# Issuing the broadcast of the layer-0 MLP gate ahead of the last two groups' query and value transfers

## The reference

```
tp = silu(cond) @ Wt + bt                     # 128 sequences x 6*128
shift_msa, scale_msa, gate_msa, shift_mlp, scale_mlp, gate_mlp = split(tp)
h = layernorm(x) * (1 + scale_msa) + shift_msa
x = x + gate_msa * attention(h)               # 16 heads of 8, 32 tokens each
h = layernorm(x) * (1 + scale_mlp) + shift_mlp
x = x + gate_mlp * (gelu(h @ W1 + b1) @ W2 + b2)
```

## Time and profile before

| | |
|---|---|
| runs | 303.29, 306.14, 344.91 us |
| span of the profiled execution | 302.6 us |
| that execution's own device time | not recorded apart; the lowest of the runs is 0.7 us above its span |
| TensorE busy | 260.4 us, 86% |
| VectorE, ScalarE, GpSimd busy | 201.6, 175.8, 185.6 us |
| DMA queue q1 | 51600 packets, 15.80 MB |
| MLP gate broadcast | four DMAs of 512 KB, 12.5 us median from issue to landing |
| V store, V read | 288 KB in 2.4 us, 72 KB in 2.6 us, medians |

### The profile page before, as it was taken

How to read it: one execution, slowest core, us unless ns; L and a number is a source line. 1 busy time by engine, 2 the same in 40 slices (tenths; PEclk the granted TensorE clock), 3 DMA queues, 4 the chain that set the end, 5 groups by cost and what they waited for, 6 DMA issues and landing times.

```text
span 302.6 us, 7656 instructions
## 1 busy us (share of the span) xinstructions
PE 260.4 (86%) x2524; PEld 201.1 (66%) x2524; DVE 201.6 (67%) x620; ACT 175.8 (58%) x366; POOL 185.6 (61%) x195
## 2 busy tenths in 40 slices
PE   0768629689999979858999999979999889999996
PEld 0556519487777766538777777858767557777776
DVE  5998964938999999816454555698999855453002
ACT  2266735646987975680555555487766696555330
POOL 5744274735687677619778788887777544445410
PEclk9999986959999999995999999999999999999999
DMA  7952766424245245670000000000000001111112
GB/s 229 320 171 33 144 107 148 90 52 85 62 66 102 61 69 98 123 140 2 1 0 0 0 0 0 2 0 2 1 0 0 1 1 37 35 35 35 35 37 69
DMA packets 52200, 18.09 MB, mean 60 GB/s; under 512 B 32464, under 2 KB 51152, under 8 KB 52048
## 3 DMA queue, kind: packets, MB, share of 16 engines
q1 hardware_dynamic: 51600, 15.80, 24.4%
q10 hardware_dynamic: 576, 1.98, 2.0%
HBM read 11.35 MB, written 4.59 MB: 53 GB/s over the span
## 4 chain that ended last, share of the span: by engine, by line
PE 50%; DMA 15%; DVE 13%; issue 7%; ACT 7%; SPq 4%; POOL 1%; DVEq 1%; ACTq 0%; POOLq 0%
PE bank L1069 20%; PE bank L931 14%; DMA values_scratch<-Vs 7%; PE bank L961 5%; DMA gate<-gates_scratch 4%; PE bank L906 3%; DMA Vx<-values_scratch 3%; ACT Kx L752 3%; DVE stats L444 2%; SPq L238 2%; SPq L253 2%; DVE hA L473 2%; PE bank L974 2%; DMA X<-x 2%; ACT xhat L737 1%
## 5 line engine op out<-in xcount | busy, mean ns | idle before, releaser
L737 ACT ACTIVATE xhat<-X,shift,rstd 128x128 f32 (+1 forms) x96 | 39.4, 483 | 56.7 <-POOL shift L294 56.6
L1069 PE MATMUL bank<-W,Qx 128*128 128x128 f32 x512 | 62.0, 282 | 0.0
L1069 PEld LDWEIGHTS bank<-W,Qx 128*128 128x128 f32 x512 | 61.0, 199 | 1.0 <-issue 1.0
L931 PE MATMUL bank<-h,W 128*128 128x512 f32 x128 | 58.5, 595 | 0.5 <-ACT Qx L787 0.5
L305 POOL TENSOR_TENSOR h<-hA,B 128x512 f32<-128x512 f32 x32 | 33.5, 1047 | 26.4 <-DVE hA L473 26.1
L473 DVE TENSOR_TENSOR hA<-bank,A 128x512 f32<-128x512 f32 x32 | 22.0, 688 | 39.5 <-PE bank L906 16.2
L787 ACT ACTIVATE Qx<-bank,col 128x512 f32<-128x512 f32 x64 | 39.3, 678 | 8.8 <-PE bank L931 8.8
L292 POOL TENSOR_TENSOR rstd<-v_sb,minus_half 128x4 f32<-128x4 f32 x32 | 32.6, 1018 | 17.8 <-DVE v_sb L464 13.2
L961 PE MATMUL bank<-Kx,Qx 128*128 128x128 f32 x256 | 37.3, 292 | 4.7 <-DVE Qx L607 1.3
L931 PEld LDWEIGHTS bank<-h,W 128*128 128x128 f32 x128 | 22.8, 191 | 22.0 <-issue 20.3
L961 PEld LDWEIGHTS bank<-Kx,Qx 128*128 128x128 f32 x256 | 32.8, 201 | 6.5 <-DMA Qx<-Qs 1.7
(11 more groups left out here) (124 smaller groups left out, 445.5 us busy)
## 6 DMA issues: line engine op xcount, KB each, us to landing
values_scratch<-Vs SPq DMA_DIRECT2D x8, 288.0 KB, 2.4
Vx<-values_scratch SPq DMA_DIRECT2D x32, 72.0 KB, 2.6
gate<-gates_scratch SPq DMA_DIRECT2D x8, 256.0 KB, 6.6
gate<-gates_scratch SPq DMA_DIRECT2D x4, 512.0 KB, 12.5
Qx<-Qs SPq DMA_DIRECT2D x28, 64.0 KB
out<-X SPq DMA_DIRECT2D x7, 256.0 KB, 2.3
W<-weights ACTq DMA_DIRECT2D x1, 1152.0 KB, 6.2
X<-x SPq DMA_DIRECT2D x4, 256.0 KB, 7.2
```

The source lines that it names most:

```text
L737: last = act.activation(xhat[:, p, P * t:P * (t + 1)], X[:, x_tile(gg, t), :], ACT.Identity, bias=shift[:, p, t:t + 1], scale=rstd[:, p, t ...
L931: last = pe.matmul(bank[2 + n][:, :], w(f"W1_{phase // 2}", n), h[:, p, :], start=True, stop=True)
L1069: last = pe.matmul(y[t // 2][:, P * t:P * (t + 1)], gT[:, p, n, P * t:P * (t + 1)], w(f"W2_{phase // 2}", n), start=(n == 0), stop=(n == N ...
```

## The change

The call that issues the MLP gate's four DMAs moves from behind the V round trip of group 7 to right behind the loop, ahead of the V round trip of group 6, the query copy of group 7 and the V round trip of group 7. Nothing else is altered: the same DMAs, waits and semaphores, and the waits for `gates_in[2]` on VectorE and GpSimd stay where they are.

```
                 spread_q(i * 2 + 4, 0)
+            spread_gates(2, 1, slice(0, NT))
             spread_v(6, 0, 3)
             spread_q(7, 1)
             spread_v(7, 1, 3)
-            spread_gates(2, 1, slice(0, NT))
```

## The result

The changed kernel takes 312.75 us (median of 4 runs, 311.0 to 313.73) against 305.3 us before (median of 4). The ratio is 1.030, 95% interval 1.025 to 1.036: slower by some 9 us. The ratio leaves out disturbed runs such as the one of 344.91 us before, and so it is not the quotient of the two medians. The forecast was 312.5 us, in a range of 305.5 to 317, slower with 0.80.

A forecast was written before the change was run, and what follows sets the result against it. V round trips were taken to bound phase 0, the MLP gate the seam, then TensorE: 14.2 us late less 6.0 regained is +8.2, span 302.6 to 310.8, with 0.7 around it 311.5; forecast 312.5 us, range 305.5 to 317.

The forecast's parts named there:

- Group 6's values come later: Late phase 0: group 6's V store waits for the gate data, landing at 117.2 instead of 104.35, 12.85 us late.
- The clock at that gap: TensorE behind the wait for group 6's values: half clock costs 2.0 us, 1.4 net of an absorbed 0.70 us wait.
- The query copy and the store of group 7 hide: End of phase 0: group 7's query copy lands by 125.5, its scores come at 127.3, so no cost.
- The seam gives back 6.0 us: Start of phase 1: the gate in time saves 3.2 us of wait and 2.8 us of slow clock.
- The sum: Whole kernel: 14.2 us late at weighting 7, less 6.0 us regained at the seam, gives 8.2 us slower.
- B: Group 6's store: only SP's 10.12 us of issue delays it, 7.1 us; kernel 2.5 us slower; chance 0.07.
- C: Group 6's store: issues take about 2.2 us, data leave it room, nothing late; kernel 6.0 us faster; chance 0.07.
- D: Seam to phase 1: something else holds its start, nothing is regained; kernel 14.2 us slower; chance 0.08.

The follow-up runs named there:

- split_late: Kernel before, with the MLP gate still behind group 7's V round trip but in two calls with a semaphore each: 297.34 us against 304.49, ratio 0.980.
- half_early: Kernel before, with half of the MLP gate issued right behind the loop, the other half behind group 7's V round trip: 304.51 us against 304.49.
- sp_held: Kernel before, with SP waiting, queue empty, ahead of group 6's V round trip until about 107.5; run again: 310.34 us against 304.01, ratio 1.024.
- act_queue: Kernel before, with the MLP gate's four DMAs on ScalarE's queue, two ahead of its group 5, two ahead of group 6: 315.45 us against 304.49.

## Why the prediction was right

It was right in its size and by its own steps, with one wrong idea of what makes the store wait.

**Group 6's values come later.** Forecast 12.85 us, measured 123.00 - 108.80 = 14.2. The term was 1.35 too small, mostly because the gate's data took 19.7 us and not 18.6 (the fourth DMA, issued at 102.35, landed 15.3 us later), while the store's lag behind them was 0.7 us as against 0.6. SP's hold was forecast at 10.12 us and was 9.83.

**The clock at that gap.** Weighting 6 to weighting 7 took 12.29 us against 11.28, so 1.0 net of the absorbed wait; forecast 1.4. The first 5.19 us (to the next group's scores) compare with 3.62, so 1.6 and not 2.0. A gap of 15.5 us cost no more clock than one of 6, as I had assumed.

**The query copy and the store of group 7 hide.** They did: the scores that need the copy did not wait, and the wait for group 7's values was 0.25 us.

**The seam gives back 6.0 us.** Measured 5.9: from weighting 7 to `hA` 13.01 us against 16.11, from `hA` to `up` 5.04 (153.34 in the chain of waits) against 7.80. It was also shown alone (split_late). What I split into 3.2 of wait and 2.8 of clock is not two separate sums: with the wait kept, the clock was worth 1.7.

**The sum.** 14.2 + 1.0 - 5.9 = 9.3 us, the difference of the spans; forecast 8.2. That 312.5 us came within 0.3 us of the median is luck, of errors that cancel. The sum was 1.1 us too small for the profiled execution, and the time around the span, 1.8 us in each of the four runs, was taken as 0.7. Against these 2.2 us stand 1.0 that I had put on top of the sum toward the high median, and 1.0 by which the profiled execution lies above the median of the four. With the 1.8 us the sum on my own terms would have been 312.6.

**The rivals.** B (only SP is held) falls by half_early, where SP is free in 2 us and the store still takes 7.8, and by sp_held, where the hold alone accounts for 6 of 14 us. C needed SP free and the data out of the store's way, and neither was so. D falls by the rows of the seam.

**What was wrong.** I wrote that a store waits for the gate data "queued before it", and thought of SP's one queue. Half of the gate on ScalarE's queue held group 6's store for as long as the same half on SP's (7.9 and 7.8 us). The figure was not touched by this, since the rows behind it held either way, but the remedy that the idea suggests cost 11 us when it was tried (act_queue).

## What to carry to other kernels

A large transfer issued early is free only if no transfer on the chain is issued while it is under way, on whatever queue; look up what the next small transfer behind it has for slack, and what the same pattern did to its neighbours elsewhere in the trace. Where a bulk transfer is waited for as a whole and only its first part is needed, split it in two with a semaphore each and leave it where it is: that took the same wait away here for nothing. What must go in between is best cut into pieces as long as the gaps. Lay out what one broadcast moves with its rows close together, in the scratch and in SBUF.

## What the runs showed of the hardware

- Two megabytes of broadcast took 19.7 us in runs of 512 B and about 13 us in runs of 16 KB with the rows closer together; for the attention gate the closer rows alone took the median from 6.6 to 5.0 us, and the longer runs from there to 4.9.
- The Trainium skill, DMA: Bandwidth & Descriptors, "Anatomy of one DMA", has 2.0 us plus bytes over 436 GB/s, an estimated 6.8 us for the 2.1 MB; neither 19.7 nor 13 comes near. The page gives that fit for DMAs that GpSimd issues, and these came from SP, so it was a weak rule to hold against the rows, in the prediction too.
- A transfer on SP's queue was held by DMAs issued on ScalarE's: a query copy's four issues took 7.00 instead of 2.6 us, a store 7.9 us to land instead of 2.4 to 3.3. The same page, "Issuing engines are not separate DMA queues", says that DMAs of different issuing engines run on the same 16 DMA engines and interleave; the trace fits that, but doesn't show whether the engines are where the time goes.
- The slow clock can come after work has begun again: in sp_held_again TensorE had waited 3.30 us at the seam, its four transposes at 143.69 still took 0.63 us, and then the stretch from 144 to 146 was granted 0.56 on the mean and the next 0.59.
- A float32 matmul call shows as two matmul instructions of 0.11 us each for 128 columns: 36 calls gave 72 instructions in 8.20 us.
